# Attention 0 with one head per full-array product: queries in zero-padded blocks, and another order of units

## The chip, the cores and the metric

One core of one Trainium2 chip runs the whole kernel as one program. The metric is the time of one execution on the device in microseconds; lower is better. Five engines work side by side, each through its own queue in the order written: TensorE (PE in the rows; its weight loads are PEld), VectorE (DVE), ScalarE (ACT), GpSimd (POOL) and SyncE (SP, which here issues DMAs). They meet through semaphores.

## The reference

32 images of 384 tokens with 192 features: 256 tokens from gathered image patches, 128 from text. Two layers follow, each an attention and a mixture of experts:

```python
h = h + attn0(layernorm(h))   # 12 heads of 16; keys = values before a layernorm; rope; latents: the last 32 tokens
h = h + ffn0(layernorm(h))    # 5 experts of 256, two chosen, all five computed
h = h + attn1(layernorm(h))   # 6 heads of 32, low-rank projections, causal
h = h + ffn1(layernorm(h))    # 8 experts of 512, two chosen, each with room for 1843 tokens
```

Attention 0 is softmax(q k / 4) times normalised keys. The first 352 tokens may look at those 352 only; the last 32 at all 384. Softmax subtracts the maximum of each row of scores.

## The kernel before, in words

The token stage does everything up to the routing of the last experts; the expert stage then runs these experts over all tokens. The change lies in the token stage. There every image passes four streams: w (embedding), x (attention 0), y (its output, and the first experts), z (attention 1 and routing). `units()` lists each stream's units, and four images are in work at a time, one in each stream. The order in which units of different streams alternate is written out by hand as a string, `ORDER`, of one letter per unit, and repeats every two images; `ORDER_OF_ONE` serves an odd one out. All engines walk through the same order, each issuing its part of every unit.

**Attention 0.** Rope leaves 12 query and 12 key heads per token. To keep precision, each is split in a rounded part and a rest; a head then fills 50 rows (three times 16, and two rows for the shift and the mask), padded to 64, so that two heads lie in one block of 128 rows. "parts" makes these, and "blocks" transposes them, a token tile of 128 at a time: 12 transposes into three banks of PSUM, two copied by ScalarE (line 845, 512 columns each) and one by VectorE (line 1338) into `heads_t`, whose first six blocks are queries and last six are keys.

"maxima" (line 942 on TensorE, line 1220 on VectorE) is a product of 128 queries and all keys for two heads, one in rows 0 to 49 and one in rows 64 to 113 of the array, each into a bank of its own; VectorE reduces each bank to a negated maximum in `neg_max`. "shift" (line 955) transposes these maxima, and ScalarE (line 855) writes them into the queries' shift row, so that the scores come out with the maximum subtracted. "score" (line 967) is the product again with keys and queries exchanged, two heads at a time; ScalarE takes exponentials (line 866). "apply" (line 985) multiplies by the values, four heads at once, each in 32 columns of the array; "group" copies the sums (line 871) and "sums" transposes them back (line 1058). Heads come in three groups of four: while one group's scores run, the next group's maxima are taken. Attention 1 does the same with heads of 97 rows, one in a block, in groups of two, and adds a causal mask by another small product (lines 948 and 973).

Banks are taken in turn, three for ScalarE's and three for VectorE's results. A fill waits until the bank's last content is read; a unit of two heads waits for both banks before its first product:

```python
banks = [fill_v("max", k, n, t, i) for i in range(2)]
```

**Around it.** The first experts' products are line 1104 (five in a row of 384 columns) and line 1113; lines 1093, 925 and 926 compute routing logits, 8 columns each; lines 915 and 1016 transpose. On GpSimd line 713 adds the two products of rope, line 707 takes the reciprocal root for the layernorms, and line 764 scatters an image's tokens to DRAM with one indirect DMA per tile and choice.

## Time and profile before

| | |
|---|---|
| Timed runs | 4501.21, 4488.57, 4482.95 us; median 4488.57 |
| Span of the profiled execution (the only time of its own that the profile gives) | 4603.4 us |
| TensorE busy | 4185.6 us, 91% |
| VectorE, ScalarE, GpSimd busy | 63%, 50%, 52% |
| Mean granted TensorE clock | 0.937 |

Busy time is the union of an engine's instructions. Matmuls overlap in the pipeline, so a matmul's own length is longer than the time for which it holds the engine; the distance between two starts says that. A granted clock of 1.00 is 2.4 GHz and 0.50 is 1.2 GHz. The profiled execution is longer than each of the timed ones.

### The profile page before, as it was taken

The numbers are of one execution on the slowest core, as the hardware profiler recorded it, in microseconds if no ns is written. First come the engines' busy times: TensorE is split into PE (matmuls) and PEld (weight loads), VectorE is DVE, ScalarE is ACT, GpSimd is POOL, SyncE is SP. The second block draws the span as 40 slices with busy tenths as digits, with TensorE's granted clock in tenths as the row PEclk, the third lists the DMA queues.
The fourth block names the chain that finished last, engine by engine and source line by source line (L and its number), as shares of the span: only waits on it lengthen the run. The fifth ranks groups of instructions, "written<-read, shape, count | busy, mean of one in ns | idle before, by whom it ended". The sixth has DMA issues, their size and how long they took to land. (4 is left out here: it accounts for less than half of the span.)

```text
span 4603.4 us, 78782 instructions
## 1 busy us (share of the span) xinstructions
PE 4185.6 (91%) x27140; PEld 3385.6 (74%) x27140; DVE 2891.6 (63%) x8103; ACT 2281.9 (50%) x5250; POOL 2372.9 (52%) x2435
## 2 busy tenths in 40 slices
PE   3899999999999999999999999999997699999999
PEld 2567777776777676777777776767676599999999
DVE  4477777777777777777777777776764333333333
ACT  1455565555555555555555555555553233333333
POOL 2355555555555555555555555555554155555555
PEclk7799999999999999999999999999998699999999
DMA  8500000000000000000000000000000122222220
GB/s 160 95 10 12 12 9 12 9 12 11 11 13 11 11 10 15 12 12 9 12 9 12 10 11 11 11 11 11 13 9 26 42 47 47 72 69 53 70 51 19
DMA packets 159100, 122.25 MB, mean 27 GB/s; under 512 B 63839, under 2 KB 150454, under 8 KB 158710
## 3 DMA queue, kind: packets, MB, share of 16 engines
q1 hardware_dynamic: 124086, 80.29, 7.8%
q0 software_dynamic: 34624, 36.92, 3.1%
q8 instruction: 226, 3.70, 0.3%
q14 instruction: 164, 1.34, 0.1%
HBM read 76.84 MB, written 74.58 MB: 33 GB/s over the span
## 5 line engine op out<-in xcount | busy, mean ns | idle before, releaser
L866 ACT ACTIVATE probs<-bank_a 128x384 f32<-128x384 f32 (+2 forms) x1728 | 692.5, 453 | 668.7 <-PE bank_a L967 436.7
L1220 DVE TENSOR_REDUCE neg_max<-bank_v 128x1 f32<-128x352 f32 (+3 forms) x1728 | 778.0, 492 | 245.2 <-PE bank_v L942 128.3
L745 POOL TENSOR_SCALAR hidden<-hidden 128x384 f32<-128x384 f32 x320 | 386.8, 1209 | 777.1 <-ACT hidden L887 775.7
L942 PE MATMUL bank_v<-heads_t 50*128 50x352 f32 (+4 forms) x1728 | 407.2, 405 | 119.1 <-DVE neg_max L1220 69.6
L985 PE MATMUL bank_o<-probs,v 128*32 128x384 f32 (+3 forms) x3456 | 455.3, 492 | 4.0 <-issue 2.6
L942 PEld LDWEIGHTS bank_v<-heads_t 50*128 50x128 f32 (+1 forms) x1728 | 210.6, 194 | 334.9 <-DVE neg_max L1220 141.2
L1533 POOL DMA_INDIRECT out_tokens<-res,token x232 | 233.0, 1005 | 372.4 <-DVE res L1718 321.2
L967 PE MATMUL bank_a<-heads_t 50*128 50x384 f32 (+3 forms) x1728 | 391.5, 392 | 30.4 <-ACT probs L866 26.2
L1104 PE MATMUL bank_a<-ffn_x,w_ffn 128*128 128x384 f32 x1600 | 390.6, 377 | 0.0
L1113 PE MATMUL bank_v<-w_down,hidden 128*128 128x192 f32 x1920 | 355.2, 335 | 5.8 <-DVE hidden L1380 4.2
L707 POOL TENSOR_TENSOR rstd<-ve,pow_half 128x3 f32<-128x3 f32 x128 | 113.0, 883 | 474.1 <-DVE ve L1156 473.8
L1104 PE MATMUL bank_v<-ffn_x,w_ffn 128*128 128x384 f32 x1600 | 356.8, 356 | 0.0
L1711 DVE TENSOR_TENSOR e_hid<-e_bank_v,gated 128x384 f32<-128x384 f32 (+1 forms) x320 | 170.8, 543 | 292.9 <-PE e_bank_v L1597 207.8
L855 ACT ACTIVATE heads_t<-bank_a 1x384 fp32r<-1x384 f32 x576 | 277.2, 481 | 154.7 <-PE bank_a L955 147.8
L747 POOL TENSOR_TENSOR hidden<-hidden 128x384 f32<-128x384 f32 x320 | 322.6, 1008 | 32.3 <-DVE hidden L1380 5.6
L1380 DVE TENSOR_TENSOR hidden<-bank_v,hidden 128x384 f32<-128x384 f32 x320 | 177.4, 554 | 254.3 <-PE bank_v L1104 254.3
L1113 PEld LDWEIGHTS bank_v<-w_down,hidden 128*128 128x128 f32 x1920 | 312.4, 192 | 33.0 <-issue 28.9
L967 PEld LDWEIGHTS bank_a<-heads_t 50*128 50x128 f32 (+1 forms) x1728 | 214.5, 196 | 161.6 <-ACT probs L866 100.3
L1617 ACT ACTIVATE gated<-e_bank_a 128x384 f32<-128x384 f32 (+1 forms) x320 | 150.2, 481 | 352.2 <-PE e_bank_a L1597 263.9
L1104 PEld LDWEIGHTS bank_a<-ffn_x,w_ffn 128*128 128x128 f32 x1600 | 288.8, 203 | 38.0 <-issue 24.0
L1104 PEld LDWEIGHTS bank_v<-ffn_x,w_ffn 128*128 128x128 f32 x1600 | 309.5, 203 | 0.0
L885 ACT ACTIVATE hidden<-bank_a 128x384 f32<-128x384 f32 x320 | 157.3, 492 | 275.5 <-issue 148.3
(246 smaller groups left out, 9308.8 us busy)
## 6 DMA issues: line engine op xcount, KB each, us to landing
xs_dram<-zeros SPq DMA_DIRECT2D x29, 780.0 KB, 18.4
rows<-xs_dram SPq DMA_DIRECT2D x232, 96.0 KB
out_tokens<-h_z SPq DMA_DIRECT2D x32, 288.0 KB, 2.3
rows<-xs_dram SPq DMA_DIRECT2D x232, 33.5 KB
hidden<-in_w SPq DMA_DIRECT2D x8, 512.0 KB
hidden<-in_w SPq DMA_DIRECT2D x16, 256.0 KB
sofar<-out_tokens,token POOLq DMA_INDIRECT x232
out_tokens<-res,token POOLq DMA_INDIRECT x232
```

What stands on the lines that cost most here:

```text
L745: step(pool.tensor_scalar(gate_tanh[:, m, :], gate_tanh[:, m, :], 1.0, None, ALU.add))
L747: pool.tensor_tensor(hid[:, e % 2, m, :], gate_tanh[:, m, :], hid[:, e % 2, m, :], ALU.mult).then_inc(hid_ready, 1)
L855: ins = act.activation(heads_t[k][to:to + 1, b, :], bank[at:at + 1, 0:T], ACT.Copy)
L866: act.activation(probs[:, n % NPROBS, i, lo:T], empty("score", k, g, kt, i)[:, lo:T], ACT.Exp, scale=DHS[k] ** -0.5).then_inc(a_free, 1)
L942: mm = pe.matmul(bank[:, 0:keys], heads_t[k][r:r + rows, b, tile[t]], heads_t[k][r:r + rows, 6 + b, 0:keys], start=True, stop=(k == 0))
L967: mm = pe.matmul(bank[:, lo:T], heads_t[k][at:at + rows, 6 + b, tile[kt]], heads_t[k][at:at + rows, b, lo:T], start=True, stop=(k == 0))
L985: mm = pe.matmul(bank_o[k][i * rows:(i + 1) * rows, lo:T], v[:, kt, PER_GROUP[k] * g + i, :], probs[:, probs_of[r, k, g, kt] % NPROBS, i, ...
L1104: mm = pe.matmul(bank[:, 0:T], w_ffn[:, wb, first:first + P], ffn_x[:, xb, :], start=(n == 0), stop=(n == len(products) - 1))
L1113: mm = pe.matmul(bank[:, 0:D], hid[:, e % 2, m, tile[t]], w_down[:, m, e, :], start=(m == 0), stop=(m == 1))
L1220: dve.tensor_reduce(neg_max[k][g % 2][:, t, at:at + 1], bank[:, 0:keys], AX.X, ALU.max, negate=True).then_inc(v_free, 1)
L1380: dve.tensor_tensor(hid[:, e % 2, m, :], bank[:, 0:T], hid[:, e % 2, m, :], ALU.mult).then_inc(v_free, 1)
L1533: pool.indirect_dma_start(out, bass.IndirectOffsetOnAxis(ap=token[:, ch, t:t + 1], axis=0), res[:, ch % NRES, t, :], None, bounds_check=N - 1,
```

## The change

A product of attention 0 now takes one head and all 128 rows of the array. The keys stay two heads to a block (`keys0`). The queries get a block for each head (`queries0`), in which the head keeps its 64 rows and the other 64 stay zero, as set once at the start; so the other head's keys add nothing. "maxima" and "score" are units of one head in both attentions, and each waits for one bank; the order within an attention alternates one maximum and one score. The blocks' copies follow: ScalarE copies a tile's queries in two halves of the array for each bank, and two blocks of keys besides. Scores of a group's first heads wait for their own shift row, not for two or four.

To make room, several tiles are smaller or shared: `rope_b` has two tile slots in place of three, `neg_max` one copy in place of two and fewer columns (97 and 33 in place of 128 and 64), `xt3` lies in `att_t`, `zeros` in `att[1]`, and small ones likewise. Third tiles of rope wait on VectorE until GpSimd has read the first one's slot, and so do the first two tiles of the next use; the first image's attention-1 output waits for the zero fill of DRAM. Both order strings are new: `ORDER` has 418 units in place of 310, as attention 0 has 36 more for each image and attention 1 has 18 more. In it the statistics of the third layernorm stand ahead of the scatters ("places") at the end of both images of a turn; before, they stood behind them in the order of the second one.

```diff
-HEAD_PARTS = (P, 3 * DH1)
-PRODUCT_ROWS = (3 * DH0 + 2, 3 * DH1)
-SCORE_ROWS = (3 * DH0 + 2, 3 * DH1 + 1)
+USED_ROWS = 3 * DH0 + 2
+PRODUCT_ROWS = (P, 3 * DH1)
+SCORE_ROWS = (P, 3 * DH1 + 1)
 SHIFT_ROW = (2 * DH0, 3 * DH1)
-SHIFT_COLS = (P, 64)
-
-
...
-        per = PER_GROUP[k] // 2
+        per = PER_GROUP[k]
         maxima = [[("maxima", k, g * per + n, t) for n in range(per) for t in range(NT)] for g in range(NGROUP[k])]
         steps = [(k, g, kt) for g in range(NGROUP[k]) for kt in range(NT)]
         out = [*maxima[0], ("shift", k, 0)]
         for n, (_, g, kt) in enumerate(steps):
-            if g + 1 < NGROUP[k]:
-                out += maxima[g + 1][kt * per:(kt + 1) * per]
-            out += [("score", *steps[n], i) for i in range(per)]
+            for i in range(per):
+                if g + 1 < NGROUP[k]:
+                    out.append(maxima[g + 1][kt * per + i])
+                out.append(("score", *steps[n], i))
             if n:
...
         rope_a = sb("rope_a", [P, NT, 2 * D])
-        rope_b = sb("rope_b", [P, NT, 2 * D])
+        rope_b = sb("rope_b", [P, 2, 2 * D])
         patches = rope_b[:, 0, 0:2 * 3 * B].rearrange("p (t n) -> p t n", t=2)
 
 
         parts = [sb(f"parts{i}", [P, 2, 6 * P], F32R) for i in range(2)]
-        heads_t = [sb(f"heads_t{k}", [P, 12, T], F32R) for k in range(2)]
-        neg_max = [[sb(f"neg_max{k}_{i}", [P, NT, SHIFT_COLS[k]]) for i in range(2)] for k in range(2)]
+        keys0 = sb("keys0", [P, H0 // 2, T], F32R)
+        queries0 = sb("queries0", [P, H0, T], F32R)
+        heads1 = sb("heads1", [P, 2 * H1, T], F32R)
+        keys_t = [keys0[:], heads1[:, H1:2 * H1, :]]
+        queries_t = [queries0[:], heads1[:, 0:H1, :]]
+        neg_max = [sb(f"neg_max{k}", [P, NT, SHIFT_COLS[k]]) for k in range(2)]
...
+        zeros = att[1][:].rearrange("p t n -> p (t n)")[:, 0:DX].unsqueeze(1)
+        ids_f = att[0][:].rearrange("p t n -> p (t n)")[:, 0:2 * B].rearrange("p (a n) -> p a n", a=2)
         att_t = sb("att_t", [KH + 1, 2, T])
...
                             pool.wait_ge(v_free, V[r, "qk", k, t] + 1)
-                            pool.tensor_tensor(rope_a[:, t, :], rope_a[:, t, :], rope_b[:, t, :], ALU.add
+                            pool.tensor_tensor(rope_a[:, t, :], rope_a[:, t, :], rope_b[:, t % 2, :], ALU.add
...
+                            if k == 0:
+                                for g in (0, 2):
+                                    bank = empty("blocks", k, t, g)[:].rearrange("p (b n) -> p b n", b=4)
+                                    first_head, pairs_here = ((0, 4), None, (8, 2))[g]
+                                    for odd in range(2):
+                                        rows = slice(odd * 64, odd * 64 + USED_ROWS)
+                                        heads = slice(first_head + odd, first_head + 2 * pairs_here, 2)
+                                        ins = act.activation(queries0[rows, heads, t * P:(t + 1) * P],
+                                                             bank[rows, 0:pairs_here, :], ACT.Copy)
+                                    if g == 2:
+                                        ins = act.activation(keys0[:, 4:6, t * P:(t + 1) * P], bank[:, 2:4, :], ACT.Copy)
+                                    ins.then_inc(a_free, 1)
+                                continue
                             for g in (0, 2):
-                                act.activation(heads_t[k][0:HEAD_PARTS[k], 4 * g:4 * g + 4, t * P:(t + 1) * P],
-                                               empty("blocks", k, t, g)[0:HEAD_PARTS[k]].rearrange(
+                                act.activation(heads1[0:PRODUCT_ROWS[1], 4 * g:4 * g + 4, t * P:(t + 1) * P],
+                                               empty("blocks", k, t, g)[0:PRODUCT_ROWS[1]].rearrange(
                                                    "p (b n) -> p b n", b=4),
                                                ACT.Copy).then_inc(a_free, 1)
                         elif what == "shift":
                             k, g = at
                             bank = empty("shift", k, g)
                             for i in range(PER_GROUP[k]):
-                                b, to = divmod((PER_GROUP[k] * g + i) * HEAD_ROWS[k] + SHIFT_ROW[k], P)
+                                head = PER_GROUP[k] * g + i
+                                to = head * HEAD_ROWS[k] % P + SHIFT_ROW[k]
                                 at = shift_column(k, i)
-                                ins = act.activation(heads_t[k][to:to + 1, b, :], bank[at:at + 1, 0:T], ACT.Copy)
-                                if k == 0 and i == 1:
-                                    ins.then_inc(shift_ready, 1)
+                                ins = act.activation(queries_t[k][to:to + 1, head, :], bank[at:at + 1, 0:T], ACT.Copy)
+                                if i < PER_GROUP[k] - 1:
+                                    ins.then_inc(shift_ready[k], 1)
                             ins.then_inc(a_free, 1)
                         elif what == "score":
-                            k, g, kt, pair = at
+                            k, g, kt, i = at
                             n = probs_of[r, k, g, kt]
-                            if n >= NPROBS and pair == 0:
+                            if n >= NPROBS and i == 0:
                                 act.wait_ge(applied, applied_of[step_of[n - NPROBS]] + 1)
                             lo = kt * P if k == 1 else 0
-                            for i in (2 * pair, 2 * pair + 1):
-                                act.activation(probs[:, n % NPROBS, i, lo:T], empty("score", k, g, kt, i)[:, lo:T],
-                                               ACT.Exp, scale=DHS[k] ** -0.5).then_inc(a_free, 1)
+                            act.activation(probs[:, n % NPROBS, i, lo:T], empty("score", k, g, kt, i)[:, lo:T],
+                                           ACT.Exp, scale=DHS[k] ** -0.5).then_inc(a_free, 1)
...
-                    def rows_of(k, hd):
-                        return hd * HEAD_ROWS[k] // P, hd * HEAD_ROWS[k] % P
-
-                    def maxima(k, n, t):
+                    def keys_of(k, rows, head):
+                        return keys_t[k][0:rows, head * HEAD_ROWS[k] // P]
+
+                    def maxima(k, head, t):
                         rows = PRODUCT_ROWS[k]
-                        if n == 0 and t == 0:
+                        if head == 0 and t == 0:
                             emptied_a("blocks", k, NT - 1, 2)
                             emptied_v("blocks", k, NT - 1, 1)
                         keys = (t + 1) * P if k == 1 else CTX if t < NT - 1 else T
-                        banks = [fill_v("max", k, n, t, i) for i in range(2)]
-                        for i, bank in enumerate(banks):
-                            b, r = rows_of(k, 2 * n + i)
-                            mm = pe.matmul(bank[:, 0:keys], heads_t[k][r:r + rows, b, tile[t]],
-                                           heads_t[k][r:r + rows, 6 + b, 0:keys], start=True, stop=(k == 0))
-                            if k == 0:
-                                mm.then_inc(v_full, 1)
+                        bank = fill_v("max", k, head, t)
+                        mm = pe.matmul(bank[:, 0:keys], queries_t[k][0:rows, head, tile[t]],
+                                       keys_of(k, rows, head)[:, 0:keys], start=True, stop=(k == 0))
                         if k == 1:
-                            for bank in banks:
-                                pe.matmul(bank[:, tile[t]], identb[:], maskq[:], start=False, stop=True
-                                          ).then_inc(v_full, 1)
+                            mm = pe.matmul(bank[:, tile[t]], identb[:], maskq[:], start=False, stop=True)
+                        mm.then_inc(v_full, 1)
 
                     def shift(k, g):
-                        emptied_v("max", k, (g + 1) * PER_GROUP[k] // 2 - 1, NT - 1, 1)
+                        emptied_v("max", k, (g + 1) * PER_GROUP[k] - 1, NT - 1)
                         bank = fill_a("shift", k, g)
                         for t in range(NT):
-                            mm = pe.transpose(bank[0:SHIFT_COLS[k], tile[t]], neg_max[k][g % 2][:, t, :], ident[:])
+                            mm = pe.transpose(bank[0:SHIFT_COLS[k], tile[t]], neg_max[k][:, t, :], ident[:])
                         mm.then_inc(a_full, 1)
 
-                    def scores(k, g, kt, n):
-                        if kt == 0 and n == 0 and k == 0:
-                            pe.wait_ge(shift_ready, NGROUP[0] * nth["x"][r] + g + 1)
+                    def scores(k, g, kt, i):
+                        per = PER_GROUP[k]
+                        if kt == 0 and i < per - 1:
+                            pe.wait_ge(shift_ready[k], (NGROUP[k] * nth["xz"[k]][r] + g) * (per - 1) + i + 1)
                         elif kt == 0:
                             emptied_a("shift", k, g)
                         rows, lo = SCORE_ROWS[k], kt * P if k == 1 else 0
-                        two = [(i, *rows_of(k, PER_GROUP[k] * g + i)) for i in (2 * n, 2 * n + 1)]
-                        banks = [fill_a("score", k, g, kt, i) for i, b, at in two]
-                        for bank, (i, b, at) in zip(banks, two):
-                            mm = pe.matmul(bank[:, lo:T], heads_t[k][at:at + rows, 6 + b, tile[kt]],
-                                           heads_t[k][at:at + rows, b, lo:T], start=True, stop=(k == 0))
-                            if k == 0:
-                                mm.then_inc(a_full, 1)
+                        head = per * g + i
+                        bank = fill_a("score", k, g, kt, i)
+                        mm = pe.matmul(bank[:, lo:T], keys_of(k, rows, head)[:, tile[kt]],
+                                       queries_t[k][0:rows, head, lo:T], start=True, stop=(k == 0))
                         if k == 1:
-                            for bank in banks:
-                                pe.matmul(bank[:, tile[kt]], identb[:], maskt[:], start=False, stop=True
-                                          ).then_inc(a_full, 1)
+                            mm = pe.matmul(bank[:, tile[kt]], identb[:], maskt[:], start=False, stop=True)
+                        mm.then_inc(a_full, 1)
 
...
                                 for b in range(4):
+                                    at = (b, 6 + b, (4, 5, 10, 11)[b])[g] if k == 0 else 4 * g + b
                                     mm = pe.transpose(bank[:, b * P:(b + 1) * P].bitcast(F32R),
-                                                      sides[:, (4 * g + b) * P:(4 * g + b + 1) * P], identr[:])
+                                                      sides[:, at * P:(at + 1) * P], identr[:])
...
+                            if t < 2:
+                                dve.wait_ge(rope_ready[k0], NT * (nth["xz"[k0]][r0] + 1) - t)
+                        if t == 2:
+                            dve.wait_ge(rope_ready[k], NT * nth["xz"[k]][r] + 1)
...
 
                     def maxima(k, n, t):
-                        g, m = divmod(n, PER_GROUP[k] // 2)
                         keys = (t + 1) * P if k == 1 else CTX if t < NT - 1 else T
-                        for i in range(2):
-                            bank = full("max", k, n, t, i)
-                            at = shift_column(k, 2 * m + i)
-                            dve.tensor_reduce(neg_max[k][g % 2][:, t, at:at + 1], bank[:, 0:keys], AX.X,
-                                              ALU.max, negate=True).then_inc(v_free, 1)
+                        bank = full("max", k, n, t)
+                        at = shift_column(k, n % PER_GROUP[k])
+                        dve.tensor_reduce(neg_max[k][:, t, at:at + 1], bank[:, 0:keys], AX.X,
+                                          ALU.max, negate=True).then_inc(v_free, 1)
...
                             k, t = at
-                            dve.tensor_copy(heads_t[k][0:HEAD_PARTS[k], 4:8, t * P:(t + 1) * P],
-                                            full("blocks", k, t, 1)[0:HEAD_PARTS[k]].rearrange("p (b n) -> p b n", b=4)
+                            rows = slice(0, PRODUCT_ROWS[k])
+                            to = (keys0[:, 0:4], heads1[rows, 4:8])[k]
+                            dve.tensor_copy(to[:, :, t * P:(t + 1) * P],
+                                            full("blocks", k, t, 1)[rows].rearrange("p (b n) -> p b n", b=4)
                                             ).then_inc(v_free, 1)
```

## Rows read from the trace of the kernel before

**Rows 1.** Page, part 1: each engine's busy us, share of the span, instructions.

```profile
PE 4185.6 (91%) x27140; PEld 3385.6 (74%) x27140; DVE 2891.6 (63%) x8103; ACT 2281.9 (50%) x5250; POOL 2372.9 (52%) x2435
```

**Rows 2.** Windows by stage: length, engines' busy us (instructions), granted clock, DMA share, GB/s.

```profile
0.00:230.00 230.00, 133.04 (x612) 90.83 (x612) 107.08 (x254) 68.16 (x147) 72.62 (x82) 0.74 0.72 127
230.00:3450.00 3220.00, 2995.57 (x20212) 2275.82 (x20211) 2350.60 (x6819) 1836.37 (x4251) 1747.49 (x1816) 0.95 0.04 11
...
3670.00:4603.00 933.00, 896.67 (x5451) 891.59 (x5449) 342.97 (x734) 310.66 (x695) 483.38 (x465) 0.98 0.21 53
```

**Rows 3.** Timeline of PE: start us, us to the last end, instructions merged.

```profile
2009.86 0.43 PE L942 MATMUL bank_v<-heads_t 50*128 50x352 f32 x2
2010.22 1.15 PE L1104 MATMUL bank_a<-ffn_x,w_ffn 128*128 128x384 f32 x5
2011.20 1.04 PE L1104 MATMUL bank_v<-ffn_x,w_ffn 128*128 128x384 f32 x5
2012.17 0.44 PE L942 MATMUL bank_v<-heads_t 50*128 50x384 f32 x2
2012.45 0.34 PE L967 MATMUL bank_a<-heads_t 50*128 50x384 f32 x2
2012.72 1.15 PE L1104 MATMUL bank_a<-ffn_x,w_ffn 128*128 128x384 f32 x5
2013.71 1.04 PE L1104 MATMUL bank_v<-ffn_x,w_ffn 128*128 128x384 f32 x5
2014.59 0.38 PE L1058 MATMUL bank_v<-ident,sums_t 128*128 128x128 f32 x2
```

**Rows 4.** Groups by line and form: busy us, mean ns, then idle before them.

```profile
L1104 PE MATMUL bank_a<-ffn_x,w_ffn 128*128 128x384 f32 x1600 | 390.6, 377 | 0.0
...
L1104 PE MATMUL bank_v<-ffn_x,w_ffn 128*128 128x384 f32 x1600 | 356.8, 356 | 0.0
...
L967 PE MATMUL bank_a<-heads_t 50*128 50x384 f32 x1152 | 247.6, 421 | 27.0 <-ACT probs L866 26.0 <-ACT heads_t L855 1.1
...
L942 PE MATMUL bank_v<-heads_t 50*128 50x352 f32 x768 | 167.8, 428 | 59.3 <-DVE neg_max L1220 42.6 <-ACT probs L866 8.1 <-ACT heads_t L845 1.0
...
L845 ACT ACTIVATE heads_t<-bank_a 128x512 fp32r<-128x512 f32 x192 | 112.6, 598 | 25.1 <-PE bank_a L1042 19.9
...
L866 ACT ACTIVATE probs<-bank_a 128x256 f32<-128x256 f32 x192 | 63.2, 381 | 63.9 <-PE bank_a L973 62.0
```

**Rows 5.** PE's waits, 230 to 3450 us: total us, times, longest.

```profile
PE bank_v L1058 <- ACT sums_t L871: 45.4, 27, 3.1
PE bank_v L942 <- DVE neg_max L1220: 42.4, 84, 0.8
PE bank_a L967 <- ACT probs L866: 16.8, 45, 0.8
```

**Rows 6.** Windows inside one turn of two images: columns as in Rows 2.

```profile
2026.40:2030.40 4.00, 3.81 (x32) 2.21 (x28) 2.90 (x7) 2.12 (x5) 2.19 (x2) 1.00 0.01 4
2030.60:2037.30 6.70, 6.70 (x26) 4.31 (x26) 3.17 (x18) 2.71 (x7) 2.17 (x2) 0.50 0.00 1
2057.90:2061.10 3.20, 2.96 (x14) 2.43 (x13) 2.23 (x8) 1.36 (x3) 1.15 (x2) 0.50 0.31 58
2143.30:2149.90 6.60, 6.60 (x26) 4.17 (x25) 4.21 (x20) 2.71 (x7) 2.37 (x3) 0.50 0.00 0
2184.20:2197.70 13.50, 13.50 (x69) 12.62 (x70) 6.97 (x26) 6.90 (x15) 6.59 (x12) 0.50 0.00 0
```

**Rows 7.** Timeline of all engines where an image ends.

```profile
2271.67 0.96 POOL L764 DMA_INDIRECT xs_dram<-xn_z,slot_i  x1 [0.31 <-issue]
...
2273.92 0.90 POOL L707 TENSOR_TENSOR rstd<-ve,pow_half 128x3 f32<-128x3 f32 x1
```

**Rows 8.** Timeline of PE ahead of the first drop of Rows 6.

```profile
2027.08 0.53 PE L915 MATMUL bank_v<-ident,xn_z 128*96 128x128 f32 x3
...
2029.56 0.37 PE L926 MATMUL bank_v<-w_g,xt 96*128 96x8 f32 x2
```

51 lines of the change are left out of this document (27 added, 24 removed).

## The prediction

> **What bounds the kernel now.** I read the engines' busy shares first, then the stages by windows, then TensorE's timeline in the middle of the run. TensorE is busy for 91% of the span, far above every other engine [rows 1]. By windows, the token stage from 230 to 3450 us holds 70% of the span: TensorE is busy for 2996 of 3220 us there, VectorE for 73%, ScalarE for 57%, GpSimd for 54%, and the DMA share is 0.04 [rows 2]. The experts' stage, 933 us, isn't touched. So a change counts by the time that it takes from TensorE's queue, by the waits in that queue, and by its clock: the mean grant is 0.95, so about 10% of the stage (2 x 0.05 x 3220 = 322 us) runs at 1.2 instead of 2.4 GHz. Since TensorE is the limit, that costs up to 161 us.
>
> The products in question are the pairs of 50-row matmuls of lines 942 and 967. Two members of a pair start together and lie in different halves of the array.
>
> **What a pair costs now, from starts on the timeline [rows 3].** Five full-array products of 384 columns that follow five others and are followed by full-array work take 2014.59 - 2013.71 = 0.88 us, 0.176 each. Five that are followed by a pair take 2012.17 - 2011.20 = 0.97 us: entering the half-array mode costs 0.09. Five that follow a pair take 2013.71 - 2012.72 = 0.99 us: leaving costs 0.11, since the first weights are no longer loaded ahead. A lone pair holds the engine for 2010.22 - 2009.86 = 0.36 us, and I take the same before an apply; two pairs in a row for 2012.72 - 2012.17 = 0.55 us, so a second one adds 0.19.
>
> The written order repeats every two images. Reading it in TensorE's sequence, I count 72 pairs in 57 runs; 40 runs are entered from full-array work and 17 from an apply (which uses column strips, a third mode); 30 leave to full-array work, 27 to an apply. Applies are entered from full-array work 8 times and left to it 18 times. Priced alike (an apply's entry and exit by the pairs' 0.09 and 0.11, an estimate), two images cost 57 x 0.36 + 15 x 0.19 + 48 x 0.09 + 48 x 0.11 = 33.0 us.
>
> **What the products cost afterwards.** Per two images 144 products: 96 of 384 columns at 0.176 and 48 of 352 columns at 0.161 (scaled by columns) make 24.6 us. All 36 applies remain; 32 are now entered from and left to full-array work: 32 x 0.20 = 6.4 us. Together 31.0, so 2.0 us less per two images, 31 us in 16 such turns. The break-even is (33.0 - 6.4) / 144 = 0.185 us per product against a mean of 0.171 here, so this is a small gain, not a large one. The other end comes from busy time per instruction: 0.244 and 0.223 us for the full-array products of line 1104, against 0.215 to 0.218 for half-array ones [rows 4]. At 0.223 (352 columns: 0.204) the 144 products cost 31.2 us and the change loses 4.6 per two images, 74 in all. I take the starts, -31, because busy intervals of pipelined matmuls overlap and the clock is mixed into them.
>
> By the Trainium skill, TensorEngine Tiling (Array Packing), section Theoretical Speedup, a contraction of at most 64 rows gains up to 2x from running two tiles at once; by that the pair should be worth nearly two products and giving it up should hurt. The pairs' 0.36 and 0.19 us in the rows come near that only for the second pair of a run.
>
> **Waits for banks.** Today a pair waits until both of its banks are free, out of three; a single head waits for one. TensorE idles 42.4 us for line 1220 before line 942 and 16.8 for line 866 before line 967 [rows 5]. VectorE's reductions and ScalarE's exponentials stay as many and as long. I take 25 of these 59 us away; the ends are -59 and, where the thinner interleaving makes them wait twice as often, +59. The largest wait, 45.4 us before the sums, longest 3.1, comes where the last apply of an image is followed at once by its sums. In the new order this stands unchanged at the end of every second image, so I keep it. What is late there besides: GpSimd's scatters, 1.27 us apart, hold back the reciprocal root until 2273.92 [rows 7]. The new order puts those statistics ahead of the scatters, but the sums' wait ends at the same place, so I count nothing for it. Six scatters of an image (7.6 us) now stand nearer to the next image's rotary additions, and the new wait at tile 2 (rope_b has two slots) makes VectorE, with everything queued behind it, wait for the first addition. Sums, transposes and the first projections lie between; without that cover I would expect 2 us per two images, 32 in all.
>
> **ScalarE.** Per tile, two copies of 512 columns (598 ns) become two copies of the same length and three of 256 (381 ns, from the 256-column exponential) [rows 4]: 1.14 us more, 3.4 per image, 110 in all. ScalarE is busy 57%, and attention-1 units and FFN stand between the last block and the first maximum, so most is hidden; the bounds are 0 and 110. I take 8, the 7% of the stage in which TensorE idles today.
>
> **Clock.** At half clock were, in one turn of two images, 6.7, 3.2, 6.6 and 13.5 us [rows 6], 30 us. Idleness isn't what they follow: before the first one TensorE was busy for 3.81 of 4.00 us at the full grant. On the timeline six transposes and twelve products of 8 columns stand there, among half-array pairs [rows 8]. Two of the four drops come at this place, the second logits of each image. The new order puts a down projection between this work and the logits in one image of two; in the other the logits still follow transposes. Removing one drop of 6.7 us would give half of it per turn, 54 in all; I take half, -27, since the new order also moves stretches whose clock I can't read. The ends are -161 (no drop left) and, 16 x 13.5 / 2 = +108, one more of the longest per turn.
>
> The Trainium skill, TensorE: Matmul & The Clock Gate, Part 4, says that transposes don't count as busy in the same way; by that the drops stay where the transposes stay, the clock term is nil and the sum is -48. That the drops follow transposes agrees with it.
>
> **Small edits.** The single neg_max and st6, vms, ohbase and zeros in other tiles add no cross-engine wait but one, once: VectorE's first attention-1 output waits for the zero fill, whose DMA load is over at 230 us (share 0.04 after it [rows 2]). The memset of the queries on GpSimd lies in the load phase (DMA share 0.72). Transposes of 97 and 33 columns load fewer weights. All nil; the memset at most 15 us by twelve 1.2 us passes, an estimate.
>
> **Sum.** -31 - 25 + 8 - 27 = -75 us on the profiled execution's 4603.4, 1.6%. The median of the timed runs, 4488.57, is 2.5% below that span, which I don't explain; scaled, 4528.4 x 4488.57 / 4603.4 = 4415 us.
>
> **Rivals.** (a) *The clock is what it's about*: full-array products fill the array's rows everywhere, and half of all low-clock time goes, -80 instead of -27. For it: two of four drops have half-array pairs beside them; against: the longest has none. -128, or 4364 us. (b) *Nothing gained*: the saved switches come back as waits, since attention-0 stretches in the new order alternate one maximum and one score and then hang on VectorE's reductions and ScalarE's exponentials one by one. For it: VectorE is at 73%; against: both have slack beside TensorE's 93%. Of the sum only the copies' 8 stay: 4496. (c) *Slower*: full-array products of changing operands don't stream at 0.176 but at 0.223 us. It decides above 0.185. Then +74 in place of -31, no wait shortened, the copies' 8, no clock gain: +82, or 4569; with the clock's -27, 4542. For it: the busy quotients; against: the starts. (d) *Packing is worth its full factor*: a pair costs 0.176 in all, and the rest of its time is something that stays. Then the change adds 72 x 0.171 = 12.3 us per turn, 197 in all, and with the other terms (-44) +153: 4638. The starts speak against it.
>
> **Chances.** Forecast 0.40 (4375 to 4460 by itself), (a) 0.18, (b) 0.20, (c) 0.18, (d) 0.04. About 0.5%, 22 us, is what a measurement of this kernel can tell from no change. Faster: forecast and (a), with a little of them lost to the middle, 0.57; same: (b), 0.21; slower: (c) and (d), 0.22. The range reaches from (a) to (c) with the clock's gain: 4350 to 4545.
>
> **What would show it.** Right: starts 0.17 to 0.18 us apart in lines 942 and 967 where full-array work surrounds them, fives behind them at 0.88 instead of 0.97 and 0.99, a grant above 0.95 in the token stage with the drop at one second-logits place gone, and less idle time before maxima and scores. Wrong: starts above 0.185, more idle time before the maxima and scores, or a stage that is no shorter although the starts are as forecast, which would put the loss in the order.

## The result, and the profile after

The changed kernel takes 4468.24 us (median of 6 runs, 4459.29 to 4474.69), the kernel before 4500.23 on the same chip (median of 6): a ratio of 0.9933, 95% interval 0.9912 to 0.9954. It is faster, as forecast, but by 0.7% where the forecast had 1.6%.

The execution of before that the forecast was counted on (span 4603.4) was an unusually slow one: nearly all timed runs lie near 4500. A further profile of the unchanged kernel (run e_before, below) has a span of 4490.0 and is what after is compared with here.

First each kernel's windows, cut at the same events: the third image's output DMA, the 29th's (26 images later), and the experts' first product. Columns as in [rows 2]. Before (e_before), then after:

```profile
0.00:523.70 523.70, 403.80 (x2491) 295.64 (x2491) 327.42 (x886) 240.42 (x546) 233.76 (x251) 0.87 0.37 61
523.70:3254.90 2731.20, 2539.95 (x17552) 1929.60 (x17550) 2040.59 (x5929) 1591.76 (x3692) 1520.88 (x1586) 0.98 0.04 12
3254.90:3584.30 329.40, 265.53 (x1582) 205.11 (x1580) 174.14 (x541) 130.13 (x307) 124.51 (x127) 0.80 0.06 18
3584.30:4490.00 905.70, 897.17 (x5520) 894.53 (x5520) 345.27 (x749) 320.40 (x705) 488.63 (x471) 0.99 0.24 58
```

```profile
0.00:505.00 505.00, 404.11 (x2561) 319.21 (x2561) 329.26 (x895) 258.98 (x604) 240.41 (x256) 0.95 0.40 63
505.00:3248.60 2743.60, 2575.68 (x17554) 2068.85 (x17550) 2019.70 (x5929) 1664.41 (x3926) 1518.86 (x1586) 0.99 0.04 12
3248.60:3552.30 303.70, 250.37 (x1514) 196.31 (x1510) 168.27 (x530) 129.46 (x303) 120.92 (x123) 0.83 0.06 19
3552.30:4457.40 905.10, 896.52 (x5520) 893.88 (x5520) 345.21 (x749) 319.60 (x705) 488.62 (x471) 0.99 0.24 58
```

The whole gain lies in the first and the last images (-18.7 and -25.7 us), where the grant is higher; the 26 images between, 61% of the time, became 12.4 us *longer* although their grant rose too. So something is given back in each image. Against the execution of [rows 2] the token stage from 230 to 3450 us goes from a grant of 0.95 to 0.99:

```profile
230.00:3450.00 3220.00, 3024.02 (x20510) 2427.42 (x20509) 2347.06 (x6889) 1938.43 (x4573) 1762.42 (x1834) 0.99 0.04 11
```

TensorE's timeline of after, with its weight loads (PEld), where maxima (L960) and scores (L982) alternate; this answers to [rows 3]:

```profile
2065.35 0.19 PEld L982 LDWEIGHTS bank_a<-queries,keys 128*128 128x128 f32 x1
2065.52 0.33 PE L982 MATMUL bank_a<-queries,keys 128*128 128x384 f32 x1
2065.52 0.19 PEld L960 LDWEIGHTS bank_v<-keys,queries 128*128 128x128 f32 x1
2065.69 0.33 PE L960 MATMUL bank_v<-keys,queries 128*128 128x384 f32 x1
...
2066.04 0.32 PE L960 MATMUL bank_v<-keys,queries 128*128 128x352 f32 x1
2066.04 0.19 PEld L982 LDWEIGHTS bank_a<-queries,keys 128*128 128x128 f32 x1
...
2066.20 0.33 PE L982 MATMUL bank_a<-queries,keys 128*128 128x384 f32 x1
2066.33 0.19 PEld L960 LDWEIGHTS bank_v<-keys,queries 128*128 128x128 f32 x1
2066.37 0.41 PE L960 MATMUL bank_v<-keys,queries 128*128 128x352 f32 x1
2066.49 0.19 PEld L982 LDWEIGHTS bank_a<-queries,keys 128*128 128x128 f32 x1
2066.61 0.35 PE L982 MATMUL bank_a<-queries,keys 128*128 128x384 f32 x1
```

As long as a product's load starts together with the product ahead of it, starts are 0.16 to 0.17 us apart and a product's record lasts 0.32 to 0.33. The load at 2066.33 starts 0.13 us after the product ahead: its product's record lasts 0.41 and the next start comes 0.24 later. No idle time is shown, since the modelled end of the matmul ahead covers the gap. Groups by form, as in [rows 4]:

```profile
L982 PE MATMUL bank_a<-queries,keys 128*128 128x384 f32 x1152 | 398.8, 370 | 14.9 <-ACT probs L886 10.1 <-ACT queries L876 2.5
...
L960 PEld LDWEIGHTS bank_v<-keys,queries 128*128 128x128 f32 x1152 | 221.8, 197 | 126.9 <-DVE neg_max L1235 61.1 <-DVE lg L1253 15.6 <-DVE hidden L1399 10.6
L982 PEld LDWEIGHTS bank_a<-queries,keys 128*128 128x128 f32 x1152 | 209.8, 189 | 87.4 <-ACT probs L886 75.9 <-ACT queries L876 5.0 <-issue 2.6
...
L858 ACT ACTIVATE queries<-bank_a 50x512 fp32r<-50x512 f32 x192 | 113.5, 591 | 17.7 <-PE bank_a L1055 15.7
...
L858 ACT ACTIVATE queries<-bank_a 50x256 fp32r<-50x256 f32 x192 | 72.6, 378 | 3.4
...
L861 ACT ACTIVATE keys<-bank_a 128x256 fp32r<-128x256 f32 x96 | 36.8, 384 | 1.1
```

TensorE's waits, as in [rows 5]:

```profile
PE bank_v L960 <- DVE neg_max L1235: 41.0, 15, 3.3
...
PE bank_v L1071 <- ACT sums_t L891: 9.2, 15, 0.6
PE bank_a L982 <- ACT probs L886: 9.1, 31, 0.4
```

And a wait of VectorE in the same window that before doesn't have:

```profile
DVE v L1222 <- POOL vrstd L762: 94.0, 30, 3.2
```

The idle time before the sums has gone from 45.4 to 9.2 us (19.0 in e_before) and that before scores from 16.8 to 9.1, but the maxima now wait 15 times, up to 3.3 us each. The timeline of all engines shows why:

```profile
2248.26 6.15 POOL L762 TENSOR_TENSOR vrstd<-vvar,pow_half 128x36 f32<-128x36 f32 x1
...
2254.45 1.05 DVE L1222 TENSOR_TENSOR v<-sums_t,vrstd 128x576 f32<-128x576 f32 x1 [3.06 <-POOL vrstd L762]
...
2255.54 0.76 DVE L1225 TENSOR_TENSOR v<-v,lng 128x576 f32<-128x576 f32 x1
...
2256.33 0.76 DVE L1228 TENSOR_TENSOR v<-v,lnb 128x576 f32<-128x576 f32 x1
...
2257.01 0.55 DVE L1235 TENSOR_REDUCE neg_max<-bank_v 128x1 f32<-128x384 f32 x1
...
2257.61 0.39 PE L960 MATMUL bank_v<-heads 96*128 96x256 f32 x1 [2.69 <-DVE neg_max L1235]
...
2258.36 0.28 ACT L886 ACTIVATE probs<-bank_a 128x128 f32<-128x128 f32 x1 [3.24 <-PE bank_a L985]
```

GpSimd's power takes 6.15 us. In the new order VectorE reaches the step that needs it (the values' last unit) 3 us too early and stands there; the reductions behind it don't free their banks, so TensorE and then ScalarE stand too.

**One account for all kernels.** For the 26 images, per image: each TensorE instruction's time from its start to the next start, less the idle time that the profile shows, at that form's mean at the full clock (issue); what the same instructions took beyond that at 1.2 GHz (clock); the shown idle time (idle). The last column is the part of issue that attention 0's products take. Median of the timed runs in front (e_before: one run).

| kernel | median us | per image | issue | clock | idle | att. 0 products |
|---|---|---|---|---|---|---|
| profile of before that was forecast on | 4500 | 107.73 | 95.94 | 4.19 | 7.60 | 12.05 |
| e_before | 4491.81 | 105.04 | 95.84 | 1.85 | 7.36 | 11.99 |
| after | 4468.24 | 105.52 | 98.12 | 0.94 | 6.46 | 16.76 |
| e_half | 4728.03 | 113.79 | 101.23 | 6.28 | 6.28 | 16.32 |
| e_old | 4501.93 | 106.21 | 96.76 | 3.33 | 6.11 | 16.87 |
| e_old_half | 4536.75 | 107.16 | 97.46 | 3.82 | 5.88 | 13.43 |
| e_pair | 4555.83 | 107.92 | 96.99 | 3.76 | 7.16 | 16.16 |
| e_values | 4420.98 | 104.25 | 98.24 | 0.56 | 5.46 | 16.95 |
| e_short | 4336.80 | 102.03 | 96.98 | 0.87 | 4.18 | 16.22 |
| e_best | 4406.58 | 103.85 | 98.54 | 0.41 | 4.90 | 17.24 |
| e_mask | 4403.41 | 103.81 | 98.48 | 0.35 | 4.98 | 17.01 |

The two profiles of before differ little in issue (95.94 and 95.84) and idle time (7.60 and 7.36) but by 2.3 us an image in the clock (4.19 and 1.85); over the whole run the first had a grant of 0.937, the second 0.956. The clock is most of why the first one was 2.5% above the median. After saves 0.9 of clock and 0.9 of idle time an image and pays 2.3 more issue, 4.8 of it on the products themselves.

### The profile page after: what moved, and what is told of

Its sections match the earlier page's. It is cut to its first block and busy times, and to the rows that moved or that the text cites. A ratio compares the mean times of both kernels' runs of the same rounds, so it can differ in the third digit from the quotient of the medians.

```text
span 4457.4 us, 78015 instructions
## 1 busy us (share of the span) xinstructions
PE 4126.7 (93%) x27140; PEld 3478.3 (78%) x27140; DVE 2862.4 (64%) x8101; ACT 2372.5 (53%) x5538; POOL 2368.8 (53%) x2436
## 5 line engine op out<-in xcount | busy, mean ns | idle before, releaser
L886 ACT ACTIVATE probs<-bank_a 128x384 f32<-128x384 f32 (+2 forms) x1728 | 705.1, 459 | 487.5 <-PE bank_a L982 279.1
L960 PE MATMUL bank_v<-keys,queries 128*128 128x352 f32 (+1 forms) x1152 | 424.5, 386 | 29.3 <-DVE lg L1253 12.8
L997 PE MATMUL bank_o<-probs,v 128*32 128x384 f32 (+3 forms) x3456 | 433.7, 473 | 0.0
L982 PE MATMUL bank_a<-queries,keys 128*128 128x384 f32 x1152 | 398.8, 370 | 14.9 <-ACT probs L886 10.1
L1117 PE MATMUL bank_v<-ffn_x,w_ffn 128*128 128x384 f32 x1600 | 337.9, 341 | 15.3 <-DVE neg_max L1235 8.1
L1117 PE MATMUL bank_a<-ffn_x,w_ffn 128*128 128x384 f32 x1600 | 347.7, 347 | 4.0 <-ACT queries L876 4.0
L1126 PEld LDWEIGHTS bank_v<-w_down,hidden 128*128 128x128 f32 x1920 | 314.1, 191 | 15.2 <-issue 12.4
L960 PEld LDWEIGHTS bank_v<-keys,queries 128*128 128x128 f32 x1152 | 221.8, 197 | 126.9 <-DVE neg_max L1235 61.1
L1117 PEld LDWEIGHTS bank_v<-ffn_x,w_ffn 128*128 128x128 f32 x1600 | 285.7, 190 | 24.8 <-DVE neg_max L1235 12.8
L1544 POOL DMA_INDIRECT sofar<-out_tokens,token x232 | 239.1, 1031 | 96.1 <-issue 74.4
L982 PEld LDWEIGHTS bank_a<-queries,keys 128*128 128x128 f32 x1152 | 209.8, 189 | 87.4 <-ACT probs L886 75.9
```

The lines of the kernel that those rows point to most:

```text
L886: act.activation(probs[:, n % NPROBS, i, lo:T], empty("score", k, g, kt, i)[:, lo:T], ACT.Exp, scale=DHS[k] ** -0.5).then_inc(a_free, 1)
L960: mm = pe.matmul(bank[:, 0:keys], queries_t[k][0:rows, head, tile[t]], keys_of(k, rows, head)[:, 0:keys], start=True, stop=(k == 0))
L982: mm = pe.matmul(bank[:, lo:T], keys_of(k, rows, head)[:, tile[kt]], queries_t[k][0:rows, head, lo:T], start=True, stop=(k == 0))
L997: mm = pe.matmul(bank_o[k][i * rows:(i + 1) * rows, lo:T], v[:, kt, PER_GROUP[k] * g + i, :], probs[:, probs_of[r, k, g, kt] % NPROBS, i, ...
L1117: mm = pe.matmul(bank[:, 0:T], w_ffn[:, wb, first:first + P], ffn_x[:, xb, :], start=(n == 0), stop=(n == len(products) - 1))
L1126: mm = pe.matmul(bank[:, 0:D], hid[:, e % 2, m, tile[t]], w_down[:, m, e, :], start=(m == 0), stop=(m == 1))
```

## The experiments

**e_before**: the kernel before, unchanged.

> The kernel before, unchanged, profiled once more: the execution that the prediction was counted on was about 100 us longer than its timed runs, at a mean granted clock of 0.937. If the timed runs of before stand at a higher clock than that profile, this one has a span near 4490 us and a mean clock of 0.95 or more, and the clock term of the change is smaller than the two profiles on hand suggest; if the clock is 0.937 again, the span is near 4600 us.

4491.81 us, span 4490.0, grant 0.956. The higher clock came, so the first profile wasn't representative.

**e_half**: the shape alone undone, in the new order.

```
-  keys_t[k][0:rows, head * HEAD_ROWS[k] // P]
+  keys_t[k][at_rows(k, rows, head), head * HEAD_ROWS[k] // P]   # rows 0 or 64, 50 of them, for attention 0
-  queries_t[k][0:rows, head, ...]
+  queries_t[k][at_rows(k, rows, head), head, ...]
```

> After, with attention 0's maxima and scores back on 50 rows (the block of queries and the keys at rows 0 or 64) in the same single-head units and the same order. Theory W (a product now carries a bank wait of its own on its weight load, so that about 100 ns of load are exposed; shape does not matter): at full clock the 50-row products keep their 0.21 to 0.25 us, and the time at half clock of the steady stage comes back from 65 us towards the 290 us of before: 4540 to 4620 us, slower than both. Rival S (the full-array shape itself streams slower than the 0.176 us that I took): the 50-row products fall to 0.17 us at full clock, some 140 us of PE time less, which pays for the clock: 4380 to 4480 us.

4728.03 us, ratio to before 1.0537 (1.0503 to 1.0570): worse than either theory. The products' issue, 16.32 us an image, is that of the full-array ones (16.76), so rival S is out: it is not the shape that makes them slow. The loss against after, 8.27 us an image, is 5.34 of clock and 3.11 of issue, all of it on other instructions than these products.

**e_old**: the new products in the order of before.

```
-  for i in range(per):
-      if g + 1 < NGROUP[k]: out.append(maxima[g + 1][kt * per + i])
-      out.append(("score", *steps[n], i))
+  if g + 1 < NGROUP[k]: out += maxima[g + 1][kt * per:(kt + 1) * per]
+  out += [("score", *steps[n], i) for i in range(per)]
...                                # and the letters of ORDER as before, x and z doubled for two heads
```

> After, with the order of units of before (each unit of two heads written as its two single-head units, back to back). Theory O (the new order costs what it hides: VectorE's last step of the values now stands right behind GpSimd's 6 us power and stalls about 3 us per turn of two images twice): with the old order the stall goes, about 45 us, and some bank waits come back, about 25 us: 4430 to 4470 us. Rival: the order is what made the change a gain; without it the time is that of before or more, 4500 to 4560 us.

4501.93 us, ratio 1.0018 (0.9999 to 1.0036): no change against before; with the other edits of the change in place, the new order is worth 0.8%. The rival holds, by another route than it said: idle time is lower than after's (6.11 to 6.46), since the 3 us stall is gone, and issue too; but the clock costs 3.33 us an image against 0.94.

A wait of this run that neither theory had comes from an edit made for room, `rope_b` with two slots. Its waits from 230 to 3450 us:

```profile
DVE rope_a L1189 <- POOL rope_a L720: 59.0, 29, 4.3
...
PE bank_v L960 <- DVE rope_b L1193: 28.3, 15, 2.1
...
PE bank_v L945 <- DVE rope_b L1193: 27.8, 15, 3.4
```

The first is VectorE waiting for GpSimd to read the shared slot. The kernel before has no such wait and after has 1.4 us of it: the new order covers it, the old one doesn't. TensorE then stands for 1.6 to 3.4 us, 26 times in the 26 images, and 126 of the 205 us at half clock begin in such a wait or within 7 us behind it. So this run doesn't show what the new products cost in the old order by themselves: the slot may take up to 50 us of idle time and 63 us of clock in it, an estimate from these rows. A run with three slots wasn't made.

**e_old_half**: both of these at once.

> The old order with single-head units, and attention 0's products on 50 rows: the fourth corner beside the full-array products in the old order (4502 us), the full-array in the new (4468) and 50 rows in the new (4728). Theory C (shape acts on the clock and on the mode switches, order on the number of switches): in the old order scores come four in a row, so there are fewer switches between products and applications than in the new order, and the loss by the 50 rows is smaller than the 260 us there: 4580 to 4680 us. Rival (the loss is the clock alone, whatever the order): about 250 us above 4502 again, 4730 to 4780 us.

4536.75 us, ratio 1.0088 (1.0054 to 1.0121): under both expectations. In the old order the shape is worth 35 us, in the new one 260. There the products of two neighbouring heads stand next to each other and mostly still overlap as in before: at the full clock the first of two scores holds TensorE for 0.042 us and the second for 0.335, 0.377 together (0.342 in e_before), against 0.47 for two full-array ones in e_old. In e_half a maximum mostly stands between two scores. Some products still overlap there, but less often: of the 1872 in the 26 images 393 start within 0.04 us of the one ahead, against 756 in e_old_half and 936 in e_before.

**e_pair**: full-array products in before's two-head units and order.

```
-  bank = fill_v("max", k, head, t)
-  mm = pe.matmul(bank[:, 0:keys], queries_t[k][0:rows, head, tile[t]], ...)
+  banks = [fill_v("max", k, head + i, t) for i in range(2)]
+  for i, bank in enumerate(banks):
+      mm = pe.matmul(bank[:, 0:keys], queries_t[k][0:rows, head + i, tile[t]], ...)
...                                # the same for the scores
```

> The kernel with after's data (zero-padded blocks of queries, full-array products) but before's units and order: two heads a unit, both banks waited for first, then the two products. Against before only the products' shape, the copies of the blocks and the place of the masks differ; against the run with the old order and single-head units (4502 us) only the sharing of the wait. Theory W (a product whose weight load has to wait for its own bank shows its load; 0.235 us in that run, 0.174 where nothing waits): the second product of each pair finds its bank free, the mean falls to 0.19 to 0.21 us, 1 to 2 us an image: 4440 to 4475 us. Rival P (waiting for two banks before either product starts later than one by one and loses what is shared): 4495 to 4530 us.

4555.83 us, ratio 1.0124 (1.0097 to 1.0152): slower than both said. That full-array products alone lose isn't shown by it: the run also has the shared slot of rope, for which VectorE waits 50.1 us and TensorE stands for 1.6 to 3.4 us 13 times in the 26 images, and attention 1's masks right behind each product. Rival P has the sign: the wait for two banks costs 1.05 us of idle time an image against e_old. Theory W's part is there too: of the 872 second products of a pair (their load waits for nothing) none had its load late, of the 873 first ones 620; but only 0.7 us an image of the products' issue came of it. By starts, a first product with a late load takes 0.263 us and one without 0.173; a second one takes 0.178 in the median and 0.212 in the mean, as the next unit's wait falls into it.

**e_values**: one unit moved.

```
+  x.remove(("values", 2))
+  x.insert(x.index(("shift", 0, 0)) + 1, ("values", 2))
```

> After, with one unit moved in each image: the last step of the values (VectorE's three products with the reciprocal root that GpSimd computes in 6 us) stands behind the first shift of attention 0 instead of right behind the last copies of the blocks; nothing else changes (the first image's one-off split of weights stays where it was). If VectorE's wait for GpSimd holds up TensorE as the trace of after shows it (2.7 to 3.3 us, once an image or once a turn): 30 waits of 3.1 us on VectorE go to near nothing and the time falls by 40 to 90 us, to 4380 to 4430 us. Rival: TensorE has other work in that stretch and the wait of the maxima for it is replaced by the next one: 4455 to 4475 us, no change.

4420.98 us, ratio to before 0.9842 (0.9811 to 0.9874). The first theory holds: VectorE's 94 us of waiting are gone, the 26 images are 33 us shorter, the span 38 us (41 by the two ratios to before). Their window:

```profile
504.60:3215.20 2710.60, 2568.66 (x17554) 2063.85 (x17550) 2026.20 (x5929) 1666.11 (x3926) 1517.14 (x1586) 0.99 0.04 12
```

**e_short**: e_values with shorter evictions. It leaves out half of attention 0's exponentials (from the third image on) and of its maxima, to free the banks sooner.

```
+  hi = T if k == 1 or nth["x"][r] < 2 else T // 2
-  act.activation(probs[:, n % NPROBS, i, lo:T], ...[:, lo:T], ...)
+  act.activation(probs[:, n % NPROBS, i, lo:hi], ...[:, lo:hi], ...)
-  dve.tensor_reduce(..., bank[:, 0:keys], ...)
+  dve.tensor_reduce(..., bank[:, 0:keys // (2 - k)], ...)
```

> The kernel with the moved values step (4421 us), with attention 0's exponentials (from the third image on) and its maxima over the first half of the columns only, so that ScalarE and VectorE free each bank about 0.2 us sooner; the products themselves are unchanged. Left out: half of the exponentials and of the maxima. Theory W (the 0.06 us by which a product exceeds 0.176 us is the wait for a bank freed late, showing the weight load): the score falls from 0.246 to 0.18 to 0.20 us and the time by 50 to 110 us, to 4310 to 4370 us. Rival L (a load that carries any wait costs its 0.06 us, whether or not the bank is free): products stay at 0.22 to 0.25 us and the time falls by less than 40 us, 4380 to 4425 us.

4336.8 us, ratio 0.9639 (0.9608 to 0.9670). The time falls as theory W says (84 us), but a score still takes 0.235 us (0.246 in e_values), as rival L says; the gain is 1.28 us of idle time and 1.26 of issue an image. So late banks are a part of it, though less work on ScalarE and VectorE shortens other waits too. Which part, a count over the products shows. In after's trace each product's wait was matched with the eviction that frees its bank; a load is late if it ends over 0.06 us after its product's recorded start (1796 products of attention 0 from 505 to 3140 us):

| after, attention 0's products | number | load late | mean us at either clock |
|---|---|---|---|
| bank free 0.1 us or more before the matmul ahead starts, that one 200 columns or longer | 958 | 3% | 0.190 |
| bank free as early, matmul ahead shorter than 200 columns (mask, down, transposes) | 326 | 100% | 0.310 |
| bank free as early, matmul ahead is an apply (32 or 64 array columns) | 126 | 100% | 0.277 |
| bank freed later | 386 | 86% | 0.271 |

In e_short the last row shrinks from 403 products (in e_values) to 241 and no other does. A bank's wait and a neighbour that is too short to hide a 0.19 us load count about alike.

**e_best**: e_values, and in every second image the unit with the patches' copies moved back.

```
   ORDER: the second image's "w" (patches), right behind values 2, to eleven letters later
```

> The kernel with the moved values step (4421 us), and in the second image of a turn the unit with the patches' copies moved from right behind that step to eleven units later. VectorE's copy waits there for GpSimd's embedding and TensorE sits idle 1.7 us before the next maxima, 13 times in 26 images. If that idle time is on the path: 10 to 27 us less, 4394 to 4411 us. Rival: the next wait takes it over, 4415 to 4425 us.

4406.58 us, ratio 0.9800 (0.9772 to 0.9828), with e_mask the fastest of those that leave nothing out, and faster than both kernels. As expected, 14 us. Its window of 26 images has the full grant:

```profile
498.80:3199.00 2700.20, 2572.82 (x17554) 2060.90 (x17550) 2026.14 (x5929) 1670.28 (x3926) 1518.45 (x1586) 1.00 0.04 12
```

**e_mask**: e_best, and a mask behind the next product rather than ahead of it.

```
-  mm = pe.matmul(bank[:, tile[t]], identb[:], maskq[:], start=False, stop=True)
+  late_masks.append((bank[:, tile[t]], maskq, v_full))   # issued behind the next product of the other ring
```

> The kernel with both moved units (4407 us), and a mask of attention 1 is issued behind the next product instead of ahead of it, where that product fills the other ring of banks: 34 of the 72 masks of a turn of two images (the others stay where they are). In its trace a product right behind a mask (0.04 us from start to start) has to show its weight load and takes 0.26 to 0.31 us instead of 0.17. Theory G (a load is hidden only by a long enough product ahead of it, whatever waits there are): 17 loads an image are hidden again, 0.06 to 0.1 us each, 1 to 1.7 us an image: 4355 to 4385 us, and the products behind a short instruction fall from 325 of 1872 to about 230. Rival W (late loads are those whose bank is freed late; a product behind a mask would be late anyway): 4395 to 4415 us.

4403.41 us, ratio 0.9810 (0.9787 to 0.9834): no change, as rival W says. Products behind a short instruction fell from 328 to 290 in the count above, those with a bank freed later rose from 404 to 430, and the hidden ones stayed. So a load that a short neighbour exposes may, behind a long one, mostly have waited for its bank. The test is a weak one: the edit took 38 products from behind a short neighbour, where 95 were expected, and at about 0.1 us each they would be worth 4 us.

## Why the prediction was wrong

The direction came about, the size didn't. Step by step:

**The step that failed is "What the products cost afterwards", -31 us.** It took for all 144 products of two images the 0.176 and 0.161 us that starts show where full-array work of one kind streams [rows 3]. Those prices exist: medians of the starts in the stretches that flow are 0.174 and 0.161 us. But only 958 of 1796 products stand so. Over all, attention 0's 72 products of an image take 16.76 us, 0.233 each, well over the 0.185 that the prediction itself had as its break-even. In place of about -1.0 us an image (31 us in 32) the issue account moved by +2.28, 59 us in the 26 images. +4.77 of that are these products; +1.20 are attention 1's, which the prediction left out; -3.69 the mode switches and waits of neighbours, so the credit for the switches was right in kind. Rival (c) had nearly this size (0.223 us) and the wrong reason: the shape streams as fast as the starts say, and e_half's half-array products are as slow in the same order. What is slow is a load of one's own behind a wait of one's own, between short neighbours.

The two prices weren't taken alike. In e_before (505 to 3249 us) the first load of a pair is late in 782 of 947 pairs, 30 an image, and such a pair takes 0.345 us, the others 0.290. In after about 45% of the products have a late load, 33 an image. So exposed loads are no more frequent than before; but the 0.36 us for a pair had one in it, and the 0.176 for a full-array product had none. Attention 1's +1.20 doesn't come from the split of its units: in e_pair, where its two heads share a unit again, its products take as long as in after (7.1 us an image, 5.9 in e_before). The masks' new place, right behind each product, is left as a reason; but e_mask, which moves 34 of 72 from there, still has 7.0, so the cause stays open.

By the Trainium skill, TensorE: Matmul & The Clock Gate, section Back-to-back issue gap, the spacing in a stream is set by the weight load and the matmul together. The count above agrees: 0.190 us where the load runs under a long matmul, 0.27 to 0.31 where it doesn't. I had read the spacing from matmuls alone.

**The stall that nothing in the sum had.** That the largest wait, the one before the sums, stands unchanged was wrong twice: the sums' wait went (19.0 us in e_before, 9.2 after), and the order brought a new one, VectorE at the 6.15 us power, with everything behind it on VectorE. It was to be read from the order: the values' last unit stood nearer to the one that starts the power. e_values shows its price, about 40 us, more than the whole measured gain.

**Waits for banks, -25.** TensorE's shown idle time fell by 0.90 us an image, 23 us in the 26 images, with the stall in it; without the stall by 1.90. That the total is near 25 is luck. The two waits that the term was about, maxima for reductions and scores for exponentials, fell from 43.8 + 18.3 us in e_before to 41.0 + 9.1 (230 to 3450 us), 12 us less, as the stall took the first one's place; in e_values they are 5.0 + 9.1. The rest came from waits that the term didn't name, such as 36.2 us at a transpose (line 1016) that waited for VectorE. What is shown as idle isn't all that a wait costs: the loads of these products still stand idle for 126.9 and 87.4 us in after, where they cost issue. They did so before, and for longer:

```profile
L942 PEld LDWEIGHTS bank_v<-heads_t 50*128 50x128 f32 x1152 | 115.6, 187 | 243.7 <-DVE neg_max L1220 109.4 <-issue 38.8 <-DVE h_y L1389 19.4
L967 PEld LDWEIGHTS bank_a<-heads_t 50*128 50x128 f32 x1152 | 114.5, 190 | 129.9 <-ACT probs L866 80.6 <-issue 41.0 <-ACT hidden L887 5.8
```

**The clock, -27.** In the 26 images it is worth 0.91 us an image against e_before, 24 us; against the slow profile that the forecast was counted on, 3.25, or 85. In the first and last images time at half clock fell from 268 to 160 us, worth up to 54, which is more than their 44 us. So a gain of rival (a)'s size came (78 us against its 80), but its mechanism, full-array products by themselves, isn't shown: e_old has them and the grant of before. I had treated (a) and (c) as exclusive, and the sizes of both came. Which half of the change does it? Summed over the clock's record of the 26 images, 1.2 GHz was granted for 113 us in e_before, 205 in e_old, 232 in e_pair, 242 in e_old_half, 328 in e_half, and 48 in after, 34 in e_values, 24 in e_best. The grants of the timed executions bear out the large differences: 0.970 to 0.975 in after, 0.952 to 0.955 in e_old, 0.947 to 0.954 in e_pair, 0.931 to 0.938 in e_half, and 0.948 to 0.970 in before. That e_old and e_pair have more than e_before isn't beyond what two executions of before differ by (259 us in the first profile). Neither half gave the gain alone, but the shape in the old order was never run without the shared slot, which has a part of these drops. At the second logits, 6.7 us at 2030.6 in [rows 6], either half is enough: drops stand there in 10 of 26 images in e_before and in 15 in e_old_half, and in none in e_old, e_pair and e_half. The order clears those at the sums and the next image's projections, which e_old still has. With half-array products the new order makes long ones of its own among masks and applies. By the Trainium skill, TensorE: Matmul & The Clock Gate, Part 4, the prediction had the drops stay where the transposes stay; here the measurement differs: in one image of two transposes still stand right before the second logits, and after shows no drop there.

**ScalarE's copies, +8.** The three rows above are 222.9 us where before's copies took 111.5: 111 more, against 110 worked out. What TensorE waits for them (7.3 us for line 858 from 230 to 3450, 1.5 for line 861) comes near the 8 that I took, by luck: that was 7% of the copies' time, and no wait was read for it. The rotary step: TensorE waits 9.7 us for its line 1193 (2.5 in e_before), where I took nothing; e_old shows what it costs without cover, about 4 us of idle time per two images where I had 2.

Together, over the 26 images: +59 issue, -24 clock, -23 idle, or +12; with -44 from the first and last images, -33 by the spans. So the direction was partly luck: in the images that the terms were worked out on, the kernel became longer, and the stages that made it faster, with more than half of the clock's gain, weren't looked at by themselves.

**What stays open.** Why the clock reacts so differently to the same half-array products in the two orders isn't settled; nor why some executions of before have twice the time at half clock. The shared slot of rope wasn't tried alone, in either order; it is the largest thing left untested, since every run but e_before has it. The zero-fill wait and the memset were not tried alone either; nothing in the traces points to them.

## What to carry to other kernels

Price a matmul with its weight load: the spacing read from a stream holds only where the load can run under a long matmul and waits for nothing; count how many instructions of the new order stand so before using it, and take both sides' prices with the same share of exposed loads. When an order of units moves, look for every step whose operand another engine takes long to make, and give it that long; here one unit moved behind the first shift was worth more than the whole change. A slot that is shared to make room brings a wait that one order covers and another doesn't: list it beside the order when runs are compared. And look at two profiles of the kernel before, if their times disagree, before counting on one.

## What the hardware showed that I hadn't expected

- Two 50-row products in different halves of the array overlap almost wholly: in e_before the second starts 0.003 to 0.007 us after the first, and both together hold TensorE for 0.33 to 0.34. Where the first load is hidden, a pair of maxima takes 0.27 us (25 pairs), against 0.35 for two full-array products at 0.174. The Trainium skill, TensorEngine Tiling (Array Packing), section Key Properties, says that tiles load and multiply in parallel; these rows agree, and of the 0.36 us that the prediction set against packing 0.09 was an exposed load.
- A load never started sooner than 0.049 us after the end of the eviction that frees its bank (1795 products of e_values).
- GpSimd's power over 36 columns takes 6.15 us, where the one over three columns took 0.90 [rows 7].
